# A two-layer transformer block on one core: the half-empty last chunk of the first MLP packed two ways, and the order of weight splits and maxima beside it

## The chip, the cores and the metric

One NeuronCore of one Trainium2 chip runs the whole program. The metric is device time in microseconds (us) of that core. The kernel before was run three times: 1961.26, 1966.72 and 1971.39 us, median 1966.72 us.

## The reference, cut to what matters

Four residual sublayers follow one another: attention with 16 heads of 128, a gated MLP, causal attention with 16 heads of 16, a mixture of experts. Each normalises its input and its output. The change lies in the second, and in the preparation of the third that runs beside it.

```
x = x + _layernorm(_L0_attn_ref(_layernorm(x), ...))
x = x + _layernorm(_L0_ffn_ref(_layernorm(x), ...))
x = x + _layernorm(_L1_attn_ref(_layernorm(x), ...))
x = x + _layernorm(_L1_ffn_ref(_layernorm(x), ...))

def _L0_ffn_ref(x, gate_w, up_w, down_w, gate_s, up_s, down_s):   # 2048 tokens, 256 features, INTER = 704
    g = jnp.einsum('th,ih->ti', xf, gate_w) * gate_s
    u = jnp.einsum('th,ih->ti', xf, up_w) * up_s
    hdn = jax.nn.silu(g) * u
    out = jnp.einsum('ti,hi->th', hdn, down_w) * down_s
```

## The kernel before, in words

Everything is fp32. A product of two fp32 tensors is done as three matmuls of rounded parts (high by high, high by low, low by high; `PASSES`, function `project`, line 81), each operand being held as a pair `_hi`, `_lo`.

The first MLP (`Mlp0.block`) works in 24 steps s = 0 to 23. Step s takes the 512 tokens of chunk c = s // 6 and the hidden units of part e = s % 6, 128 at a time. The 704 hidden units are five parts of 128 and one of 64: for e = 5 (steps 5, 11, 17 and 23) the other 64 units are zeros. Within a step:

- TensorE, `gate_up(s)`: 6 matmuls of 512 columns for the gate into one PSUM bank, 6 for the up projection into the next (line 81).
- ScalarE, `silu(s)` (L1369): 128x512, as soon as the gate is there.
- VectorE, `product(s)` (L1451): silu times up, 128x512.
- ScalarE, `split_hidden(s)` (L1376): the high part `mlp_hid_hi`.
- GpSimd (L1426): the low part `mlp_hid_lo`.
- TensorE, `down(s)`: 8 matmuls of 256 columns with the high part (L1333), then 4 with the low part (L1337), added up in two banks of PSUM over the six steps of a chunk. Step 0 of a chunk first writes zeros into the banks (L1330).

TensorE issues `gate_up(s + 1)` ahead of `down(s)`, so that the other engines have the time of `gate_up(s + 1)` to make the hidden values of step s.

```
gate_up(0)
for s in range(STEPS):
    gate_up(s + 1)
    early.tensor(pe, s, 0)
    down(s)
    turn(...)                  # X_TURN, NEXT_TURN
    early.tensor(pe, s, 1)
```

Each engine runs its program in the order of the code. Other work is set into the steps by tables: the norm before (`before`: X_ADD, X_STATS, X_ACT, X_TURN), the norm after (`after`: NEXT_ACC, NEXT_ADD, NEXT_STATS, NEXT_X_ACT, NEXT_TURN), the splits of the MLP's own weights (`SPLIT`, L1362 on ScalarE and L1417 on GpSimd), and class `Early`, which prepares the next attention. For this text the following of it count:

- On GpSimd, `Early.gpsimd` splits weights into high and low parts: in step 6 those of query and key (`split_weights`), in step 8 both halves of the value weights (`halve`, L2015 and L2017), in steps 9 and 11 those of the output weights (L2148, L2151). In step 8 they follow `scale_x` of the norm (L216 to L221).
- In steps 16 to 23 TensorE computes the first scores of the next attention just for their row maxima (`early_jobs`, L2058 with the mask L2065, 64 rows each, in pairs over the two halves of the array), and VectorE reduces them (`take_max`, L2091 and L2094; here called peaks). Two banks are used in turn, so that each pair of scores waits for the peaks before it. "when" 0 stands ahead of `down(s)`, "when" 1 behind it.
- VectorE does the peaks of step s - 1 in its pass s (`early.vector(dve, s - 1)`), behind `product(s)` and behind `take_lo` (L379), which takes the low part of a tile that TensorE has transposed (`turn`, L365) and of which ScalarE has first taken the high part (L370).

## Time and profile before

| | |
|---|---|
| runs | 1961.26, 1966.72, 1971.39 us |
| the profiled execution's own time | 1961.52 us |
| its span | 1959.7 us, mean granted clock of TensorE 0.985 |
| TensorE matmuls busy | 1864.2 us (95%) |
| TensorE weight loads busy | 1471.1 us (75%) |
| VectorE busy | 1429.8 us (73%) |
| ScalarE busy | 1176.6 us (60%) |
| GpSimd busy | 1173.6 us (60%) |

The program is a sequence of stages: the first attention to about 1135 us of the span, the first MLP from there to about 1271 us, then the second attention and the experts. The page's rows of engine activity are means over slices of 49 us, so the MLP is less than three of them; it has to be read in finer stretches. Matmul durations in the trace include the time that a matmul takes to run through the array: consecutive ones overlap, and what one costs in a row of them is the distance from start to start.

### The profile page before, as it was taken

Reading aid. Unit: us, or ns where it says so; the run is one execution under the profiler, and the core shown is the slowest. Engines: PE = TensorE matmul, PEld = TensorE weight load, DVE = VectorE, ACT = ScalarE, POOL = GpSimd, SP = SyncE. Lnnn points to the kernel's source line nnn. Section 1 sums busy time; section 2 is a strip of 40 time slices with the busy share of each in tenths; the row PEclk is TensorE's granted clock in tenths of the full one; section 3 lists DMA queues with packets and bytes.
Section 4 is the critical chain, followed back from the end, with each engine's and each line's share of the span. In section 5 each row is a group of like instructions: output and inputs, shape, how many; then the busy total and the mean of one; then the engine's idle time right before and its main releaser. Section 6 shows DMA issues by size and latency. Waiting matters only on the chain. (4 is left out here: it accounts for less than half of the span.)

```text
span 1959.7 us, 31266 instructions
## 1 busy us (share of the span) xinstructions
PE 1864.2 (95%) x10576; PEld 1471.1 (75%) x10576; DVE 1429.8 (73%) x2312; ACT 1176.6 (60%) x1897; POOL 1173.6 (60%) x945
## 2 busy tenths in 40 slices
PE   6999999999999999999999699889999989999997
PEld 5778888888888888888888577654555546888886
DVE  7777888888888888888888644377777766655556
ACT  5666676666666766666666655257666765533333
POOL 3776776777777767867766665214434446554445
PEclk9999999999999999999999899989999999999999
DMA  7877777778677777777777420000000010110001
GB/s 210 278 256 265 269 269 280 256 270 283 246 271 275 264 260 258 268 283 259 269 271 260 159 87 1 2 12 4 4 4 4 2 49 25 41 41 25 17 1 44
DMA packets 195603, 310.68 MB, mean 159 GB/s; under 512 B 12080, under 2 KB 154160, under 8 KB 195504
## 3 DMA queue, kind: packets, MB, share of 16 engines
q1 hardware_dynamic: 195504, 309.39, 45.9%
q8 instruction: 59, 0.97, 0.2%
q14 instruction: 40, 0.33, 0.1%
HBM read 173.03 MB, written 136.31 MB: 158 GB/s over the span
## 5 line engine op out<-in xcount | busy, mean ns | idle before, releaser
L620 POOL TENSOR_TENSOR attn_probT_lo<-attn_probT_lo,attn_probT_hi 128x1024 fp32r<-128x1024 f32 x254 | 610.6, 2404 | 198.4 <-ACT attn_probT_hi L987 198.1
L1104 DVE STREAM_TRANSPOSE attn_turned_prob<-attn_prob 128x1024 f32<-128x1024 f32 x256 | 318.2, 1243 | 123.9 <-ACT attn_prob L977 65.2
L977 ACT ACTIVATE attn_prob<-psum,attn_neg_max 128x1024 f32<-128x1024 f32 x256 | 285.7, 1116 | 145.2 <-DVE attn_neg_max L1098 142.0
L1098 DVE TENSOR_REDUCE attn_neg_max<-psum 128x1 f32<-128x1024 f32 x256 | 305.8, 1195 | 18.6 <-PE psum L81 18.0
L987 ACT ACTIVATE attn_probT_hi<-attn_probT_lo 128x1024 fp32r<-128x1024 f32 x256 | 269.3, 1052 | 2.2 <-DMA attn_probT_lo<-attn_spill 2.1
L81 PE MATMUL psum<-attn_probT_hi,attn_v_hi 128*128 128x512 f32 x512 | 205.5, 401 | 21.9 <-POOL attn_probT_lo L620 20.2
L81 PE MATMUL psum<-attn_probT_lo,attn_v_hi 128*128 128x512 f32 x512 | 205.3, 401 | 0.0
L81 PE MATMUL psum<-attn_key_hi,attn_q_hi 128*128 128x512 f32 x512 | 200.6, 392 | 3.8 <-ACT attn_prob L977 2.2
L81 PE MATMUL psum<-attn_probT_hi,attn_v_lo 128*128 128x512 f32 x512 | 203.6, 398 | 0.0
L81 PE MATMUL psum<-attn_key_lo,attn_q_hi 128*128 128x512 f32 x512 | 201.9, 394 | 0.0
L81 PE MATMUL psum<-attn_key_hi,attn_q_lo 128*128 128x512 f32 x512 | 201.2, 393 | 0.0
L2094 DVE TENSOR_REDUCE attn_peaks<-psum 128x1 f32<-128x512 f32 (+1 forms) x256 | 156.0, 652 | 45.3 <-PE psum L2065 30.0
L1718 POOL TENSOR_TENSOR attn_qk_lo<-attn_moe_hidden,attn_qk_hi 128x512 fp32r<-128x512 f32 (+1 forms) x73 | 93.6, 1282 | 142.8 <-ACT attn_qk_hi L1660 142.8
L2546 ACT ACTIVATE attn_probT<-psum 128x512 f32<-128x512 f32 (+1 forms) x256 | 129.1, 574 | 40.6 <-PE psum L2428 34.9
L830 POOL TENSOR_TENSOR attn_v_lo<-attn_v_whole,attn_v_hi 128x512 fp32r<-128x512 f32 x64 | 83.3, 1301 | 104.0 <-ACT attn_v_hi L999 103.7
L1747 DVE TENSOR_TENSOR attn_moe_hidden<-psum,attn_v 128x512 f32<-128x512 f32 (+1 forms) x73 | 49.8, 683 | 115.5 <-ACT attn_v L1653 109.0
L81 PEld LDWEIGHTS psum<-attn_probT_hi,attn_v_hi 128*128 128x128 f32 x512 | 97.0, 189 | 44.3 <-issue 14.4
L81 PEld LDWEIGHTS psum<-attn_key_hi,attn_q_hi 128*128 128x128 f32 x512 | 96.6, 189 | 29.2 <-ACT attn_prob L977 3.5
L2364 POOL TENSOR_SCALAR_AFFINE_SELECT attn_probT<-attn_probT 128x256 f32<-128x256 f32 x128 | 52.0, 420 | 110.7 <-ACT attn_probT L2546 56.7
L81 PE MATMUL psum<-xT_hi,attn_w_hi 128*128 128x512 f32 x288 | 116.6, 405 | 1.4 <-ACT attn_probT L2546 0.5
L81 PE MATMUL psum<-xT_hi,attn_w_lo 128*128 128x512 f32 x288 | 114.7, 398 | 0.0
L81 PEld LDWEIGHTS psum<-attn_probT_hi,attn_v_lo 128*128 128x128 f32 x512 | 97.1, 190 | 23.5
(251 smaller groups left out, 4761.1 us busy)
## 6 DMA issues: line engine op xcount, KB each, us to landing
attn_spill<-attn_turned_prob SPq DMA_DIRECT2D x256, 512.0 KB, 4.5
attn_probT_lo<-attn_spill SPq DMA_DIRECT2D x256, 512.0 KB, 5.0
x_sb<-in_w_qkvo SPq DMA_DIRECT2D x30, 512.0 KB, 5.0
attn_v_all<-in_moe_w SPq DMA_DIRECT2D x24, 384.0 KB, 3.0
acc_sb<-in_x SPq DMA_DIRECT2D x4, 512.0 KB, 6.1
acc_sb<-in_bo SPq DMA_DIRECT2D x16, 128.0 KB, 6.9
x_sb<-in_x SPq DMA_DIRECT2D x4, 512.0 KB, 5.5
mlp_staged<-in_ffn_w SPq DMA_DIRECT2D x4, 384.0 KB, 4.9
```

The costliest lines, as they stand in the source:

```text
L81: ins = nc.tensor.matmul(out, stationary[s], moving[m], start=start and n == 0, stop=stop and n == len(PASSES) - 1)
L620: engine.tensor_tensor(lo, f32(lo), f32(hi), ALU.subtract).then_inc(done, 1)
L830: nc.gpsimd.tensor_tensor(v[1][:, to, cols], v_whole[:, to, cols], f32(v[0][:, to, cols]), ALU.subtract).then_inc(v_done, 1)
L977: nc.scalar.activation(prob[:, tile % 2, :].rearrange("p (b n) -> p b n", b=NSQ), by_key, ACT.Exp, bias=neg_max[:, tile % 2:tile % 2 + 1], ...
L987: nc.scalar.activation(hi, f32(lo), ACT.Copy).then_inc(hi_done, 1)
L1098: nc.vector.tensor_reduce(neg_max[:, tile % 2:tile % 2 + 1], scores(tile), AX.XY, ALU.max, negate=True).then_inc(max_ready, 1)
L1104: nc.vector.transpose(turned_prob[:, tile % 2, :], prob[:, tile % 2, :]).then_inc(turned, 1)
L1718: self.nc.gpsimd.tensor_tensor(self.hid[1][p % 2][:, at], self.hidden[p % 2][:, at], f32(self.hid[0][p % 2][:, at]), ALU.subtract).then_in ...
L1747: self.nc.vector.tensor_tensor(self.hidden[p % 2][:, at], self.k.psum[:, self.slots[p % 2][1], at], self.gate_act[p % 2][:, at], ALU.mult) ...
L2094: nc.vector.tensor_reduce(to[:, h:h + 1], bank[:, 0:width], AX.X, ALU.max, negate=True).then_inc(max_free, 1)
L2364: nc.gpsimd.affine_select(out=at, in_=at, pattern=[[0, 2], [1, P]], compare_op=ALU.is_ge, fill=0.0, base=0, channel_multiplier=-1).then_in ...
L2546: nc.scalar.activation(probT[:, slot(g, h), q0:], score_bank(g, h), ACT.Exp, scale=float(D1) ** -0.5).then_inc(exp_done, 1)
```

## The change

Three things are changed.

1. In the steps with e = 5 (`narrow`), gate and up weights of the 64 units stand side by side in one stationary of 128 columns. The first 256 tokens of the chunk go through [gate, up] into one bank, the other 256 through [up, gate] into the other: 12 matmuls of 256 columns. Silu and product are each done in two instructions of 64x256, the product reading the up values in the other half of the partitions than the one it writes. The hidden values of the first 256 tokens then lie in partitions 0 to 63, of the other 256 in 64 to 127, in 256 columns; the split into high and low is 128x256. The down projection has 12 matmuls of 64 rows, alternately in the upper and the lower half of the rows, each pair into the two banks.
2. On GpSimd the value weights are split in steps 9 and 11, the output weights in steps 12 and 14.
3. On VectorE the peaks of the "when" 0 scores come ahead of `take_lo`, and in a narrow step ahead of the product.

```diff
@@ Mlp0.block
+        HALF_NB = NB // 2
+        sides = (slice(0, P // 2), slice(P // 2, P))
+        narrow = lambda s: part_of(s) == N - 1
@@ gate_up
+                    if narrow(s):
+                        for half, (cols_of, full) in enumerate(((gates, gate_full), (ups, up_full))):
+                            at = slice(c * NB + half * HALF_NB, c * NB + (half + 1) * HALF_NB)
+                            project(nc, banks[:, half, 0:HALF_NB], cols_of, lambda kt: [h[:, kt, at] for h in k.xT]).then_inc(full, 1)
+                        return
@@ down
+                def narrow_down(c, buffer, weights, lo_of):
+                    for j in range(GT // 2):
+                        for of, weight in ((0, 0), (0, 1)) if lo_of is None else ((lo_of, 0),):
+                            for side in range(2):
+                                mm = nc.tensor.matmul(down_tile(c, side * GT // 2 + j), hid[of][sides[side], buffer, j * P:(j + 1) * P],
+                                                      weights[weight][sides[side], :], start=False, stop=of == 1 and j == 1)
+                    return mm
+                    if narrow(s):
+                        narrow_down(c, s % 2, weights, lo_of=None)
+                        pe.wait_ge(lo_done, s + 1)
+                        narrow_down(c, s % 2, weights, lo_of=1).then_inc(down_full, 1)
+                        return
@@ silu
+                    if narrow(s):
+                        for side in range(2):
+                            if side:
+                                act.wait_ge(up_full, s + 1)
+                            nc.scalar.activation(gate_act[sides[side], s % 2, 0:HALF_NB],
+                                                 slot(("step", s))[sides[side], side, 0:HALF_NB], ACT.Silu,
+                                                 scale=scales[sides[side], 0, e:e + 1]).then_inc(silu_done, 1)
+                        return
@@ product
+                    if narrow(s):
+                        e = part_of(s)
+                        for side in range(2):
+                            dve.wait_ge(silu_done, silus_before(s) + side + 1)
+                            mul = nc.vector.scalar_tensor_tensor(out=hidden[sides[side], s % 2, 0:HALF_NB],
+                                                                 in0=slot(("step", s))[sides[1 - side], side, 0:HALF_NB],
+                                                                 scalar=scales[sides[side], 1, e:e + 1],
+                                                                 in1=gate_act[sides[side], s % 2, 0:HALF_NB], op0=ALU.mult, op1=ALU.mult)
+                        mul.then_inc(prod_done, 1)
+                        return
@@ VectorE, pass s
+                    if narrow(s):
+                        early.vector(dve, s - 1, 0)
                     product(s)
...
                     if s - 1 in X_TURN:
                         before.take_lo(dve, X_TURN[s - 1], slot(("x", X_TURN[s - 1])))
+                    if not narrow(s):
+                        early.vector(dve, s - 1, 0)
                     if s - 1 in NEXT_TURN:
                         after.take_lo(dve, NEXT_TURN[s - 1], slot(("next", NEXT_TURN[s - 1])))
-                    early.vector(dve, s - 1)
+                    early.vector(dve, s - 1, 1)
@@ Early.gpsimd
-                if step == 8:
+                if step == 9:
                     pool.wait_ge(wv_landed, 32)
-                    halve(pool, wv_in[:], [flat(h[:]) for h in wv], wv_ready, 2)
-                if step == 9:
+                    nc.gpsimd.tensor_tensor(flat(wv[0][:]), wv_in[:], one[:].broadcast_to([P, KC * C]), ALU.mult).then_inc(split, 1)
+                if step == 11:
+                    pool.wait_ge(split, 2)
+                    nc.gpsimd.tensor_tensor(flat(wv[1][:]), wv_in[:], f32(flat(wv[0][:])), ALU.subtract).then_inc(wv_ready, 1)
+                if step == 12:
                     nc.gpsimd.tensor_tensor(flat(wp[0][:]), wp_in[:], one[:].broadcast_to([P, passes // 2 * C]), ALU.mult).then_inc(split, 1)
-                if step == 11:
+                if step == 14:
```

The weights are arranged on the host, outside the measured time: the last chunk of `ffn0_w` holds [gate, up], [up, gate] and the 64 rows of down twice, and its scales stand in both halves.

**GpSimd, steps 8 to 11.** `mlp_hid_lo` is the low part of a step's hidden values; the four `room_sb` rows are `scale_and_offset` of a norm. Before:

```order
L216 TENSOR_SCALAR room_sb<-room_sb 128x4
L217 TENSOR_SCALAR room_sb<-room_sb 128x4
L219 TENSOR_TENSOR room_sb<-room_sb 128x4
L221 TENSOR_TENSOR room_sb<-room_sb 128x4
L2015 TENSOR_TENSOR attn_wv_hi<-attn_in_wv,attn_one 128x512
L2017 TENSOR_TENSOR attn_wv_lo<-attn_in_wv,attn_wv_hi 128x512
L1426 TENSOR_TENSOR mlp_hid_lo<-mlp_hidden,mlp_hid_hi 128x512
L2148 TENSOR_TENSOR attn_wp_hi<-attn_in_wp,attn_one 128x512
L1426 TENSOR_TENSOR mlp_hid_lo<-mlp_hidden,mlp_hid_hi 128x512
```

and now (L1458 is L1426 of before, L2193 makes the high part of the value weights, L2196 the low part):

```order
L221 TENSOR_TENSOR room_sb<-room_sb 128x4
L1458 TENSOR_TENSOR mlp_hid_lo<-mlp_hidden,mlp_hid_hi 128x512
L2193 TENSOR_TENSOR attn_wv_hi<-attn_in_wv,attn_one 128x512
L1458 TENSOR_TENSOR mlp_hid_lo<-mlp_hidden,mlp_hid_hi 128x512
L216 TENSOR_SCALAR room_sb<-room_sb 128x4
L217 TENSOR_SCALAR room_sb<-room_sb 128x4
L219 TENSOR_TENSOR room_sb<-room_sb 128x4
L221 TENSOR_TENSOR room_sb<-room_sb 128x4
L1458 TENSOR_TENSOR mlp_hid_lo<-mlp_hidden,mlp_hid_hi 128x256
L2196 TENSOR_TENSOR attn_wv_lo<-attn_in_wv,attn_wv_hi 128x512
```

The low part of step 9 no longer has two splits ahead of it, and that of step 11 has 256 columns.

**VectorE, steps 17 to 19.** Before, where L1451 is the product, L379 is `take_lo` and L2091 and L2094 are peaks:

```order
L2091 TENSOR_REDUCE attn_peaks<-psum 128x2 x2
L2094 TENSOR_REDUCE attn_peaks<-psum 128x1 x2
L1451 SCALAR_TENSOR_TENSOR mlp_hidden<-psum,mlp_in_scales,mlp_gate_act 128x512
L379 TENSOR_TENSOR xT_lo<-psum,xT_hi 128x2x512
L2094 TENSOR_REDUCE attn_peaks<-psum 128x1 x4
```

and now (L2138 and L2141 are the peaks, L1485 the two halves of a narrow product, L1493 a whole one):

```order
L2138 TENSOR_REDUCE attn_peaks<-psum 128x2 x2
L1485 SCALAR_TENSOR_TENSOR mlp_hidden<-psum,mlp_in_scales,mlp_gate_act 64x256 x2
L2141 TENSOR_REDUCE attn_peaks<-psum 128x1 x2
L1493 SCALAR_TENSOR_TENSOR mlp_hidden<-psum,mlp_in_scales,mlp_gate_act 128x512
L2141 TENSOR_REDUCE attn_peaks<-psum 128x1 x2
L379 TENSOR_TENSOR xT_lo<-psum,xT_hi 128x2x512
L2141 TENSOR_REDUCE attn_peaks<-psum 128x1 x2
```

Two of the four peaks that stood behind `take_lo` now stand ahead of it, and the first pair stands ahead of the product of step 17.

**TensorE, step 5.** The down projection of a narrow step now (L1333 is `narrow_down`; "x2" is one matmul in each half of the rows). Before, these were 8 and 4 single matmuls over all 128 rows:

```order
L1333 MATMUL psum<-mlp_w_hi,mlp_hid_hi 128x256 x2
L1333 MATMUL psum<-mlp_w_lo,mlp_hid_hi 128x256 x2
L1333 MATMUL psum<-mlp_w_hi,mlp_hid_hi 128x256 x2
L1333 MATMUL psum<-mlp_w_lo,mlp_hid_hi 128x256 x2
L1333 MATMUL psum<-mlp_w_hi,mlp_hid_lo 128x256 x4
```

There are as many matmuls as before, in six pairs.

## Rows read from the trace of the kernel before

**Rows 1.** Busy time by stretch: us, each engine's busy time, TensorE's granted clock, DMA
```profile
1235.00:1240.00 5.00, 4.57 (x15) 3.39 (x16) 1.40 (x3) 0.69 (x1) 0.00 (x0) 0.50 0.00 0
...
1290.00:1300.00 10.00, 9.62 (x63) 6.31 (x65) 4.90 (x10) 6.65 (x12) 2.68 (x5) 0.66 0.00 0
```

**Rows 2.** Timeline, TensorE, steps 9 and 10: start us, us, engine, line, what
```profile
1180.37 0.40 PE L81 MATMUL psum<-xT_hi,mlp_w_hi 128*128 128x512 f32 x1
...
1182.94 0.40 PE L81 MATMUL psum<-xT_hi,mlp_w_lo 128*128 128x512 f32 x1
1183.17 0.28 PE L1333 MATMUL psum<-mlp_w_hi,mlp_hid_hi 128*128 128x256 f32 x1
...
1184.00 0.28 PE L1333 MATMUL psum<-mlp_w_lo,mlp_hid_hi 128*128 128x256 f32 x1
```

**Rows 3.** Timeline, GpSimd, step 4
```profile
1158.66 1.84 POOL L1417 TENSOR_TENSOR mlp_w_lo<-x_sb,mlp_w_hi 128x768 fp32r<-128x768 f32 x1
```

**Rows 4.** Timeline, TensorE, into matmuls of 64 rows and back (PEld: weight loads)
```profile
1212.87 0.64 PE L1337 MATMUL psum<-mlp_w_hi,mlp_hid_lo 128*128 128x256 f32 x4
1213.44 0.19 PEld L2039 LDWEIGHTS psum<-attn_qk_hi,attn_to_stack 64*128 64x128 f32 x2
1213.44 0.50 PE L2039 MATMUL psum<-attn_qk_hi,attn_to_stack 64*128 64x512 f32 x2
1213.78 0.40 PE L2039 MATMUL psum<-attn_qk_lo,attn_to_stack 64*128 64x512 f32 x2
1214.11 0.50 PE L81 MATMUL psum<-xT_hi,mlp_w_hi 128*128 128x512 f32 x1
1214.45 0.40 PE L81 MATMUL psum<-xT_lo,mlp_w_hi 128*128 128x512 f32 x1
```

**Rows 5.** Timeline, GpSimd and TensorE, step 9
```profile
1182.85 2.11 POOL L2015 TENSOR_TENSOR attn_wv_hi<-attn_in_wv,attn_one 128x512 fp32r<-128x512 f32 x1
1185.04 1.27 POOL L2017 TENSOR_TENSOR attn_wv_lo<-attn_in_wv,attn_wv_hi 128x512 fp32r<-128x512 f32 x1
1186.27 1.27 POOL L1426 TENSOR_TENSOR mlp_hid_lo<-mlp_hidden,mlp_hid_hi 128x512 fp32r<-128x512 f32 x1
...
1187.59 0.74 PE L1337 MATMUL psum<-mlp_w_hi,mlp_hid_lo 128*128 128x256 f32 x4 [3.32 <-POOL mlp_hid_lo L1426]
```

**Rows 6.** Timeline, ScalarE, steps 9 and 10
```profile
1184.91 0.67 ACT L1369 ACTIVATE mlp_gate_act<-psum,mlp_in_scales 128x512 f32<-128x512 f32 x1
1186.40 0.63 ACT L1376 ACTIVATE mlp_hid_hi<-mlp_hidden 128x512 fp32r<-128x512 f32 x1 [0.82 <-DVE mlp_hidden L1451]
```

**Rows 7.** Groups of instructions in the MLP, GpSimd: count, busy us, mean ns, idle before
```profile
L1426 POOL TENSOR_TENSOR mlp_hid_lo<-mlp_hidden,mlp_hid_hi 128x512 fp32r<-128x512 f32 x24 | 32.4, 1349 | 54.3 <-ACT mlp_hid_hi L1376 54.1
```

**Rows 8.** Timeline, VectorE, steps 18 and 19
```profile
1228.77 0.75 DVE L1451 SCALAR_TENSOR_TENSOR mlp_hidden<-psum,mlp_in_scales,mlp_gate_act 128x512 f32<-128x512 f32 x1 [1.77 <-ACT mlp_gate_act L1369]
...
1232.96 1.23 DVE L379 TENSOR_TENSOR xT_lo<-psum,xT_hi 128x1024 fp32r<-128x1024 f32 x1 [3.44 <-ACT xT_hi L370]
1234.10 1.28 DVE L2094 TENSOR_REDUCE attn_peaks<-psum 128x1 f32<-128x512 f32 x2
```

**Rows 9.** Timeline, TensorE, steps 17 and 18: scores for maxima, then gate of step 19
```profile
1225.04 0.50 PE L2058 MATMUL psum<-attn_key,attn_q 64*128 64x512 f32 x2 [0.40 <-DVE attn_peaks L2091]
...
1235.43 0.69 PE L2058 MATMUL psum<-attn_key,attn_q 64*128 64x384 f32 x2 [3.70 <-DVE attn_peaks L2094]
...
1236.29 0.79 PE L81 MATMUL psum<-xT_hi,mlp_w_hi 128*128 128x512 f32 x1
...
1240.88 0.40 PE L81 MATMUL psum<-xT_hi,mlp_w_lo 128*128 128x512 f32 x1
```

**Rows 10.** Groups of instructions in the MLP, VectorE: count, busy us, mean ns
```profile
L2094 DVE TENSOR_REDUCE attn_peaks<-psum 128x1 f32<-128x512 f32 x8 | 5.1, 685 | 2.4 <-PE psum L2058 1.6 <-PE psum L2065 0.7
...
L2091 DVE TENSOR_REDUCE attn_peaks<-psum 128x2 f32<-128x256 f32 x2 | 0.7, 416 | 0.0
```

**Rows 11.** Timeline, TensorE, last step
```profile
1267.80 0.50 PE L2058 MATMUL psum<-attn_key,attn_q 64*128 64x512 f32 x2 [1.38 <-DVE attn_peaks L2094]
```

More of the change, by code:

```diff
@@ L1241, in block @@
         chunk_of = lambda s: s // N
+        HALF_NB = NB // 2
+        sides = (slice(0, P // 2), slice(P // 2, P))
+        narrow = lambda s: part_of(s) == N - 1
+        tokens_of = lambda s: HALF_NB if narrow(s) else NB
+        silus_before = lambda s: s + s // N
         X_ADD, X_STATS, X_ACT, X_TURN = {3: 2, 7: 3}, {4: 2, 8: 3}, {5: 2, 9: 3}, {7: 2, 11: 3}
@@ L1313, in gate_up @@
                     banks = slot(("step", s))
-                    project(nc, banks[:, 0, :], lambda kt: weights(slice(kt * IM, (kt + 1) * IM)),
-                            x).then_inc(gate_full, 1)
-                    project(nc, banks[:, 1, :], lambda kt: weights(slice(cols_up + kt * IM, cols_up + (kt + 1) * IM)),
-                            x).then_inc(up_full, 1)
+                    gates = lambda kt: weights(slice(kt * IM, (kt + 1) * IM))
+                    ups = lambda kt: weights(slice(cols_up + kt * IM, cols_up + (kt + 1) * IM))
+                    if narrow(s):
[3 more added lines that the diff above has]
+                        return
+                    project(nc, banks[:, 0, :], gates, x).then_inc(gate_full, 1)
+                    project(nc, banks[:, 1, :], ups, x).then_inc(up_full, 1)
+                def narrow_down(c, buffer, weights, lo_of):
[5 more added lines that the diff above has]
+                    return mm
                 def down(s):
@@ L1375, in split_hidden @@
                         act.wait_ge(down_full, s - 1)
-                    nc.scalar.activation(hid[0][:, s % 2, :], hidden[:, s % 2, :], ACT.Copy).then_inc(hi_done, 1)
+                    nc.scalar.activation(hid[0][:, s % 2, 0:tokens_of(s)], hidden[:, s % 2, 0:tokens_of(s)], ACT.Copy).then_inc(hi_done, 1)
                 def copy_out(c):
@@ L1425, in _ @@
                     pool.wait_ge(hi_done, s + 1)
-                    nc.gpsimd.tensor_tensor(hid[1][:, s % 2, :], hidden[:, s % 2, :], f32(hid[0][:, s % 2, :]),
+                    of = slice(0, tokens_of(s))
+                    nc.gpsimd.tensor_tensor(hid[1][:, s % 2, of], hidden[:, s % 2, of], f32(hid[0][:, s % 2, of]),
                                             ALU.subtract).then_inc(lo_done, 1)
@@ L1479, in _ @@
                         after.stats_x(dve, NEXT_STATS[s])
-                early.vector(dve, STEPS - 1)
+                for when in range(2):
+                    early.vector(dve, STEPS - 1, when)
 class Moe:
@@ L2200, in scalar, with vector @@
                             take_stack(act, 0, n, part, bank)
-            def vector(self, dve, step):
-                if step == 8:
+            def vector(self, dve, step, when):
+                if step == 8 and when == 0:
                     dve.wait_ge(consts, 64)
@@ L2210, in vector @@
                     dve.wait_ge(prepared, 2)
-                for job in self.done_in(step):
+                for job in early_jobs.get(step, ((), ()))[when]:
                     kind, n, part = job
@@ L2764 @@
                               pad_hidden(given["L0_ffn_down_w"].T))
+    last, own = arrays["ffn0_w"][-1], IM // 2
+    in_gate, in_up = (last[:, n * KC * IM:(n + 1) * KC * IM].reshape(P, KC, IM)[:, :, 0:own] for n in range(2))
+    arrays["ffn0_w"][-1] = np.concatenate([
+        np.concatenate([in_gate, in_up], axis=2).reshape(P, -1), np.concatenate([in_up, in_gate], axis=2).reshape(P, -1),
+        np.concatenate([last[0:own, 2 * KC * IM:], last[0:own, 2 * KC * IM:]])], axis=1)
     arrays["ffn0_scales"] = np.stack([pad_hidden(given[f"L0_ffn_{n}_s"]).reshape(N_FFN0, IM).T for n in ("gate", "up")])
+    arrays["ffn0_scales"][:, own:, -1] = arrays["ffn0_scales"][:, 0:own, -1]
     arrays["down_s"] = given["L0_ffn_down_s"]
```

4 lines of the change are left out of this document (2 added, 2 removed).

## The prediction

> **What bounds the kernel now.** The page comes first, and says little here: TensorE's matmuls are busy 95% of the span, and the change touches the MLP alone, 136 us of it. I read that stage by stretches of 5 us. TensorE has 5.00 us busy in most of them, and the exceptions are what a reader should look for: a wait in step 9, one in step 17 with a granted clock of 0.50 behind it [rows 1], and short waits at the end. Then the timeline of TensorE. Twelve matmuls of 512 columns run from 1180.37 to 1182.94, (2.57 / 11 =) 0.234 us each from start to start; eight of 256 columns from 1183.17 to 1184.00, (0.83 / 7 =) 0.119 each [rows 2]. These distances, not the durations of 0.40 and 0.28 in the same rows, are what a matmul costs. A step is 12 x 0.234 + 12 x 0.119 = 4.2 us of TensorE, and as long as nothing is late TensorE is the bound of this stage. So the sum is TensorE time removed, plus waits removed, minus waits that appear.
>
> All positions below are those of the trace of before.
>
> **A, gate and up.** Each narrow step has 12 matmuls of 256 instead of 512 columns: 12 x (0.234 - 0.119) = 1.4 us, four times 5.5. One small loss: gate and up of step 6 need weights whose low part ends on GpSimd at 1158.66 + 1.84 = 1160.50 [rows 3]; TensorE would now be there at 1160.35. 0.2 is taken off: **5.3 us**.
>
> **B, down.** Six pairs instead of twelve matmuls. That two matmuls of 64 rows run side by side is in the trace: the pair at 1213.44 (row x2) is followed by the next at 1213.78, and that one by the next matmul at 1214.11, so two times 512 columns take 0.33, which two in turn (0.47) would not fit into. Both weight loads of a pair are over in 0.19, the length of one [rows 4]. So 6 x 0.119 = 0.71 is saved. Against it stands going from 128 rows to 64 and back. The four matmuls at 1212.87 should be followed after 4 x 0.119 at 1213.34, the pair starts at 1213.44; the next follows after 0.34 rather than 0.234: 0.10 + 0.10. On the way back 0.33 and 0.34 stand for 0.234 again. One change of size costs 0.20 [rows 4]. Steps 5 and 11 gain such a change in both directions: 0.71 - 0.41 = 0.3 each. In steps 17 and 23 the scores ahead of the down are of 64 rows already, so the change moves behind the down in 17 (0.71) and falls away in 23 (0.9). Sum **2.2 us**. Bounds: 3.0 gained, if the change of size were hidden; 0.6 lost, if the pairs ran in turn (2.2 - 4 x 0.71). I take the value by the pairs of 512 columns, the nearest row.
>
> The rule in the Trainium skill, TensorEngine Tiling (Array Packing), Key Properties, is that changing the tiling mode drains TensorE; it gives no price. It speaks against part B, and the trace agrees with 0.20 a time. The same skill's TensorE: Matmul & The Clock Gate, LDWEIGHTS, says that a load costs its columns, whatever its rows: 107 ns for 128 columns by its formula, an estimate, so that pairs whose two loads came one after the other would cost 0.21 and B would be nothing.
>
> **C, the value weights.** The low part of step 9 starts at 1186.27, behind splits of 2.11 and 1.27 us, and TensorE waits 3.32 [rows 5]. Without them GpSimd gets to it when the norm's small work ends, at 1182.85, and is done at 1184.12; TensorE wants it at 1184.00 + 0.12 [rows 2]. The 3.3 go. Next late is step 10. Its silu starts at 1184.91, because the norm's work on ScalarE stands ahead of it; its high part is done at 1186.40 + 0.63 = 1187.03 [rows 6]. That chain moves with TensorE, which is 1.5 earlier by then (1.2 + 0.3 of step 5): 1185.5. TensorE, after down(9) ending at 1183.1 and a gate and up of step 11 of only 1.4, is there at 1184.5: it waits 1.0, and about 0.4 more for the low part, which needs 1.27 [rows 5] where the high matmuls give 0.95 of cover. **3.3 - 1.4 = 1.9 us.** Before, the wait for step 9 hid this. The splits that move to steps 9, 11, 12 and 14 take 1.3 to 2.1 each; GpSimd idles 54.3 us ahead of the 24 low parts, over 2 us a step [rows 7], and in step 11 its own low part is half as long; nobody reads them before the next stage. Cost nothing; if one fell ahead of a low part that TensorE awaits, at most 1.3 each.
>
> **D, the maxima.** VectorE ends the product of step 18 at 1229.5 and then stands 3.44 in front of `take_lo`, until the transposed tile's high part is there; the peaks behind it were ready all along, end at 1235.4, and TensorE waits 3.70 for them [rows 8, 9]. Now they run from 1229.5 to 1230.8, when TensorE is still in the transposes: 3.6 go. Behind the wait the granted clock was 0.50 of full, the lower level of 1.2 GHz [rows 1]: gate and up of step 19 took from 1236.29 to 1240.88, 0.417 a matmul for 0.234 [rows 9], and the scores ahead of them 0.86 to the next start for 0.65. That gives back 2.0 + 0.2. Peaks before the product of step 17 also take away the 0.40 in front of the second scores [rows 9]. What is late next: the peaks behind `take_lo`, which down(18) needs. After the turn come the high part (1.0), `take_lo` (1.23) and peaks of 384 columns (1.0, between the two rows of peaks), while TensorE has 0.65 of scores and 2.8 of gate and up: no wait, by some 0.2. **6.2 us.**
>
> **E, the small engines.** Two half products for one: by the nearest row of a half-width reading of PSUM, 416 ns against 685 [rows 10], about 0.5 each for 0.75 [rows 8]: 0.2 more on VectorE; two half silus, 0.3 more on ScalarE, less 0.2 for the shorter high part; GpSimd is relieved of 0.6 a step. Bounds: 0.37 and 0.75 per half. The cover is gate and up of the wide step that follows, 2.8 us, which stays. Step 23 has only the scores' wait as cover [rows 11], where VectorE is free before the scores are. **0.**
>
> **The sum** is 5.3 + 2.2 + 1.9 + 6.2 = 15.6 us. What lies behind the MLP starts on a barrier and moves forward as a whole. The profiled execution took 1961.5 us, so 1945.9 by its own time; the median of the three runs lies 5.2 above. I take the median less the sum, **1951 us**.
>
> What no row can fix: where the half-level stretches behind the MLP fall. 1290 to 1300 is at 0.66 [rows 1]: (1.00 - 0.66) x 2 = 0.68 of the time at half speed, at most 3.4 us of cost. Everything arrives there 15.6 us earlier, so up to 4 more or less.
>
> **The rivals.**
>
> 1. *The pairs run in turn.* Pairs of 512 columns speak against it [rows 4]; with 256 each load has half the time to hide in. B becomes -0.6, the time 1954. By the skill's rule on loads it would be 1953. Chance 0.10.
> 2. *The clock falls anyway.* The new wait of 1.4 us in step 10, or the shorter work of the narrow steps, puts a stretch at half speed elsewhere. For it: in this stage 3.7 us of wait was enough; against: the wait of 3.32 in step 9 was followed by no fall. One or two such stretches cost 2.2 each, one behind the stage up to 3.4: 1953 to 1957, say 1956. Chance 0.15.
> 3. *The cover is gone.* In each narrow step the others have 1.4 us less to bring the hidden values of the step before, and TensorE waits where it computed: all of A is given back except what C has counted. 15.6 - 3.9 = 11.7, 1955. For it: step 10, where I find it. Against: VectorE and ScalarE idle before their part of most steps. Chance 0.12.
> 4. *Slower.* Half-filled matmuls, two a pair with 64 rows each, keep TensorE so little occupied that the granted clock goes to its lower level from the first narrow step on. Work of X us at full clock then costs X more, so the gain is used up when 15.6 us of work, some 31 us of the stage, run at 0.50. If all the work from step 5 to the end did, about 95 us, it would be 1951 + 95 = 2046 us. Against it: the downs of 256 columns keep their 0.119 at full clock [rows 2], and the narrow downs are 4 x 1 us. The point for slower by over 0.5% is 51 us at 0.50. Chance 0.03.
>
> That the change does not do what it says has little room: the order of instructions shows six pairs and the moved peaks; what is left is rival 1.
>
> **How the numbers follow.** My forecast has 0.60. Before's three runs lie 0.5% apart, which is also what a measurement of this kernel can tell from no change: faster by over 0.5% is below 1956.9. Of the forecast 0.55 falls there (the sum would have to be off by 6 us), of rival 1 0.09, of 2 0.09, of 3 0.08: 0.81. Slower 0.03, the rest 0.16. The range takes the sum with the unfixed 4 us and the lowest of the runs downwards (1961.3 - 19.6 = 1942), and upwards rivals 1 to 3 with the bounds: 1960.
>
> **What would show it.** Matmuls of 256 columns on line 81 in four groups of 12 at 0.119; down of a narrow step in 1.1 us; no wait of TensorE for the low part of step 9, but one of 1 to 1.4 in step 10; no wait of several us between the transposes of step 17 and the next scores, and a clock of 1.00 there; the MLP 15 to 16 us shorter from its first matmul to the barrier. A MLP shortened by less than 11, or a clock of 0.50 inside it, makes the sum wrong; a MLP shortened as said with the time elsewhere makes the whole wrong and the parts right.

## The result, and the profile after

The changed kernel takes 1946.63 us, the median of four runs (1943.77 to 1950.39), beside 1969.06 (1961.26 to 1974.59) for four of the kernel before; the ratio is 0.9888, interval 0.9866 to 0.991. Run again on another chip it takes 1951.99 beside 1967.88, ratio 0.9906, 0.9883 to 0.9928. Forecast were 1951 and a range of 1942 to 1960.

| | before | after |
|---|---|---|
| the profiled execution's own time | 1961.52 us | 1944.76 us |
| span, mean granted clock | 1959.7, 0.985 | 1943.0, 0.987 |
| first matmul of the MLP to gate of step 5 | 22.28 | 23.44 |
| gate of step 5 to the barrier | 113.78 | 98.30 |
| ahead of the MLP, behind it | 1135.2, 688.5 | 1134.9, 686.4 |

The last three lines come from the timelines; the MLP's first matmul starts at 1135.19 us before and at 1134.85 after. Of the kernel after, the first narrow matmul on TensorE, and SyncE's first transfer behind the barrier that ends the MLP:

```profile
1158.29 0.36 PE L81 MATMUL psum<-xT_hi,mlp_w_hi 128*128 128x256 f32 x1 [0.32 <-issue]
...
1256.59 0.33 SPq L2374 DMA_DIRECT2D attn_sum_rows<-in_sum_rows  x1
```

The kernel before has the same two points in its timeline:

```profile
1157.47 0.47 PE L81 MATMUL psum<-xT_hi,mlp_w_hi 128*128 128x512 f32 x1 [0.23 <-issue]
...
1271.25 0.33 SPq L2324 DMA_DIRECT2D attn_sum_rows<-in_sum_rows  x1
```

98.30 for 113.78 is **15.5 us less, where the sum said 15.6**. This distance, called the changed stretch below, holds all that the change touches. It is also the steady measure: in the second execution of the change it is 98.33. What lies around it is the same code in both kernels and varies by itself: the MLP starts at 1134.5 to 1139.1 in the profiled executions, its head takes 22.2 to 22.3 us in most of them and 23.4 to 23.6 in others, whatever the kernel, and what lies behind takes 686.4 to 694.3.

The whole MLP, for which the prediction named 15 to 16 us less, went from 136.1 to 121.7, so 14.3 shorter; in the second execution it is 120.6, 15.5 shorter. The first one's head stands in part at the lower clock, ahead of everything that the change touches:

```profile
1135.00:1140.00 5.00, 5.00 (x16) 3.94 (x17) 3.10 (x10) 1.36 (x2) 3.94 (x8) 0.66 0.83 274
```

The kernel before and the second execution have 1.00 in their heads. The five engine values in such a row are the busy times of TensorE, its weight loads, VectorE, ScalarE and GpSimd; the number behind them is the granted clock.

The waits of TensorE in the changed stretch, in the kernel before (us in total, times, longest):

```profile
PE psum L2058 <- DVE attn_peaks L2094: 5.1, 2, 3.7
PE psum L1337 <- POOL mlp_hid_lo L1426: 3.3, 1, 3.3
...
PE psum L2058 <- DVE attn_peaks L2091: 0.4, 1, 0.4
```

and in the kernel after (L2141 is L2094 of before, L1458 is L1426):

```profile
PE psum L2105 <- DVE attn_peaks L2141: 1.4, 1, 1.4
PE psum L1360 <- POOL mlp_hid_lo L1458: 1.1, 2, 0.9
```

3.3 and 3.7 us of wait are gone. What has come is 1.1 us for GpSimd's low parts. In windows of 5 us the stretch behind the scores of steps 17 and 18, which answers to the 0.50 of [rows 1], stands at full clock:

```profile
1225.00:1230.00 5.00, 4.85 (x27) 3.35 (x25) 2.90 (x4) 3.06 (x4) 0.72 (x1) 1.00 0.00 0
1230.00:1235.00 5.00, 5.00 (x38) 3.84 (x38) 1.27 (x3) 0.89 (x2) 1.29 (x1) 1.00 0.00 0
```

The timeline of TensorE in step 5 has the narrow down, where a wide step has eight single matmuls ([rows 2] show them) and four. The row ahead is the last of gate and up of step 6, the rows behind are the first of step 7:

```profile
1164.00 0.40 PE L81 MATMUL psum<-xT_hi,mlp_w_lo 128*128 128x512 f32 x1
1164.33 0.39 PE L1333 MATMUL psum<-mlp_w_hi,mlp_hid_hi 64*128 64x256 f32 x2
1164.55 0.28 PE L1333 MATMUL psum<-mlp_w_lo,mlp_hid_hi 64*128 64x256 f32 x2
1164.67 0.28 PE L1333 MATMUL psum<-mlp_w_hi,mlp_hid_hi 64*128 64x256 f32 x2
1164.79 0.28 PE L1333 MATMUL psum<-mlp_w_lo,mlp_hid_hi 64*128 64x256 f32 x2
1164.90 0.40 PE L1333 MATMUL psum<-mlp_w_hi,mlp_hid_lo 64*128 64x256 f32 x4
1165.23 0.50 PE L81 MATMUL psum<-xT_hi,mlp_w_hi 128*128 128x512 f32 x1
1165.57 0.39 PE L81 MATMUL psum<-xT_lo,mlp_w_hi 128*128 128x512 f32 x1
```

Read the distances of starts: 0.12 from pair to pair. Four distances are about 0.1 longer than their matmuls ask, two on the way in (0.33 for 0.234, 0.22 for 0.119) and two on the way out (0.33 for the last two pairs' 0.24, 0.34 for 0.234). From 1164.00 to 1165.57 there are 1.57 us; two matmuls of 512 columns are 0.47 of it, so the down costs 1.10. Before it was 12 x 0.119 = 1.43.

The timelines of GpSimd and VectorE in step 9, and TensorE's two waits:

```profile
1180.45 1.53 POOL L219 TENSOR_TENSOR room_sb<-room_sb 128x4 f32<-128x4 f32 x1
1182.06 0.20 POOL L221 TENSOR_TENSOR room_sb<-room_sb 128x4 f32<-128x4 f32 x1
1182.21 2.34 POOL L1458 TENSOR_TENSOR mlp_hid_lo<-mlp_hidden,mlp_hid_hi 128x512 fp32r<-128x512 f32 x1
...
1182.20 1.23 DVE L275 TENSOR_TENSOR x_sb<-x_sb,acc_sb 128x1024 f32<-128x1024 f32 x1
```

```profile
1184.61 0.74 PE L1360 MATMUL psum<-mlp_w_hi,mlp_hid_lo 128*128 128x256 f32 x4 [0.94 <-POOL mlp_hid_lo L1458]
...
1187.87 0.74 PE L1360 MATMUL psum<-mlp_w_hi,mlp_hid_lo 128*128 128x256 f32 x4 [0.15 <-POOL mlp_hid_lo L1458]
```

GpSimd starts the low part as forecast, right behind the norm's small work. But it takes 2.34 us for the 1.27 of [rows 5], while VectorE's addition of 1.23 us (L275) runs beside it.

The trace of before had a sign of this. There the same addition ran beside the first split, whose 2.11 us stand in [rows 5], and an operation of the same kind and shape without the addition beside it took half of that:

```profile
1182.84 1.22 DVE L275 TENSOR_TENSOR x_sb<-x_sb,acc_sb 128x1024 f32<-128x1024 f32 x1
...
1187.50 1.04 POOL L2148 TENSOR_TENSOR attn_wp_hi<-attn_in_wp,attn_one 128x512 fp32r<-128x512 f32 x1
```

### The profile page after: what moved, and what is told of

Read it like the earlier page. It is cut to its first block and busy times, and to the rows that moved or that the text cites. A ratio compares the mean times of both kernels' runs of the same rounds, so it can differ in the third digit from the quotient of the medians.

```text
span 1943.0 us, 31274 instructions
## 1 busy us (share of the span) xinstructions
PE 1855.7 (96%) x10576; PEld 1463.3 (75%) x10576; DVE 1431.3 (74%) x2316; ACT 1175.5 (60%) x1901; POOL 1169.9 (60%) x945
## 5 line engine op out<-in xcount | busy, mean ns | idle before, releaser
L2141 DVE TENSOR_REDUCE attn_peaks<-psum 128x1 f32<-128x512 f32 (+1 forms) x256 | 155.9, 651 | 44.4 <-PE psum L2112 29.8
L81 PEld LDWEIGHTS psum<-attn_probT_hi,attn_v_lo 128*128 128x128 f32 x512 | 97.2, 190 | 23.6
L81 PE MATMUL psum<-xT_hi,attn_q 128*128 128x512 f32 x288 | 114.6, 398 | 0.0
```

Source lines behind the costliest of these rows:

```text
L81: ins = nc.tensor.matmul(out, stationary[s], moving[m], start=start and n == 0, stop=stop and n == len(PASSES) - 1)
L2141: nc.vector.tensor_reduce(to[:, h:h + 1], bank[:, 0:width], AX.X, ALU.max, negate=True).then_inc(max_free, 1)
```

## The experiments

Each is measured in the changed stretch too, against the change's 98.3.

**The change once more.** Edit: none.

> The change as it is, once more beside the kernel before. In the profiles the first MLP (first matmul to the start of the next stage's first transfer) went from 136.1 to 121.7 us and the span by 16.7, yet the medians differ by 22.4. Theory 1: the change is worth its sum of 15.6 and about 1 us more, the rest is scatter of the kernel before: ratio 0.9915, 16 to 18 us. Theory 2: about 5 us more come from outside of the MLP: ratio 0.9888, and the stretch behind the MLP is shorter by over 4 us.

1951.99 us, ratio 0.9906 (0.9883 to 0.9928), nearer to the first theory's 0.9915 than to the second's 0.9888; changed stretch 98.33. So the stretch repeats within 0.1 us, while the two profiled executions differ by 8 us in all: 4.3 ahead of the MLP, 4.7 behind it, and 1.2 the other way in its head. For what lies behind, windows of both show a difference: the change's first profile, then this one, each 1260 to 1300.

```profile
1260.00:1300.00 40.00, 33.84 (x268) 20.25 (x268) 30.12 (x61) 24.25 (x45) 7.34 (x16) 1.00 0.06 13
```

```profile
1260.00:1300.00 40.00, 34.67 (x240) 22.77 (x240) 27.88 (x55) 18.37 (x33) 7.38 (x16) 0.87 0.08 15
```

A granted clock of 1.00 or 0.87 over 40 us, for one and the same program, is up to 0.13 x 40 = 5.2 us, enough for the 4.7. What made the 4.3 ahead of the MLP stays open.

**Part 1 undone: the last 64 units as before.**

```diff
-        narrow = lambda s: part_of(s) == N - 1
+        narrow = lambda s: False
+        last_part = lambda s: part_of(s) == N - 1
...
-        silus_before = lambda s: s + s // N
+        silus_before = lambda s: s
```

The peaks keep their places of part 3 (by `last_part` instead of `narrow`), and the weights' old arrangement comes with it.

> Part 1 of the change undone (last 64 units as a full chunk with zeros), parts 2 and 3 kept. The sum says A + B = 5.3 + 2.2 = 7.5 us longer than the change; the MLP lasts 121.7 + 7.5 = 129 us, TensorE waits in steps 9 and 10 as long as in the change (1.1 in all) or less. Rival, cover gone: the narrow steps are bounded by the other engines, so that undoing them costs under 5 us.

1956.45 us, ratio 0.9938 (0.9917 to 0.996); changed stretch 105.90, 7.6 more than the change. That looks like A + B, which was 7.5, to the tenth, and isn't quite. In the last 4 us before the barrier this execution has a low clock, which the change has not:

```profile
1260.05:1262.05 2.00, 2.00 (x12) 1.78 (x11) 1.29 (x2) 0.00 (x0) 0.00 (x0) 0.70 0.00 0
1262.05:1264.05 2.00, 0.68 (x4) 0.39 (x2) 0.00 (x0) 1.02 (x1) 0.00 (x0) 0.50 0.00 0
```

From the last scores to the barrier are 4.21 us, in the kernel before, at full clock, 3.45 (1267.80 to 1271.25): 0.8 of the 7.6 are clock, and 6.8 the change's own. Followed step by step from the gate of step 5, the two timelines part by 1.4 at each narrow gate and up of steps 17 and 23, by 0.7 at the down of 17, 0.9 at that of 23, 1.45 over step 5, all as forecast, but by 0.96 over step 11 where 1.7 was forecast. 0.3 of what is missing is the low part of step 10, which C has counted. Most of the rest is a wait of 0.35 that only the change has, on the weight loads ahead of the matmuls behind the turn of step 11:

```profile
1196.56 0.19 PEld L81 LDWEIGHTS psum<-xT_hi,mlp_w_hi 128*128 128x128 f32 x1 [0.35 <-DVE mlp_hidden L1493]
```

(second execution of the change). Gate and up of step 13 need the banks that VectorE's product of step 12 still reads.

This run also has 0.9 us of wait for the low part of step 9, as the change has: that wait does not come from the narrow steps.

**Part 2 undone: the value and output weights split in steps 8, 9 and 11.**

```diff
-                if step == 9:
+                if step == 8:
                     pool.wait_ge(wv_landed, 32)
-                    nc.gpsimd.tensor_tensor(flat(wv[0][:]), wv_in[:], one[:].broadcast_to([P, KC * C]), ALU.mult).then_inc(split, 1)
-                if step == 11:
...
+                    halve(pool, wv_in[:], [flat(h[:]) for h in wv], wv_ready, 2)
+                if step == 9:
```

> Part 2 undone (value weights split whole in step 8, output weights in 9 and 11). TensorE waits 3 to 4 us for the low part of step 9 again instead of 0.94, and no longer in step 10: 2 to 3 us longer than the change, MLP 124 us. Rival: the wait comes back but narrow steps behind it take it up, under 1 us.

1956.15 us, ratio 0.9934 (0.9915 to 0.9953); changed stretch 101.59, 3.3 more. TensorE's timeline and the windows behind the wait:

```profile
1189.12 1.17 PE L1360 MATMUL psum<-mlp_w_hi,mlp_hid_lo 128*128 128x256 f32 x4 [3.45 <-POOL mlp_hid_lo L1458]
```

```profile
1185.00:1190.00 5.00, 1.55 (x10) 1.34 (x9) 2.17 (x6) 3.28 (x6) 4.92 (x5) 0.92 0.00 0
1190.00:1195.00 5.00, 5.00 (x31) 4.83 (x29) 1.68 (x8) 2.08 (x5) 3.62 (x7) 0.74 0.00 0
```

A wait of 3.45 for 1.09 is 2.4 of the 3.3. The clock fell behind this wait: the two rows lose up to 1.7 us to it, and by the starts of both timelines it cost 1.5. In all, by the starts, 3.3 is 2.5 for the wait in step 9 and 1.5 for the clock, less 0.4 in step 10 and the product's 0.35, which the longer wait covers. In the kernel before the clock had not fallen behind 3.32.

**Part 3 undone: the peaks behind `take_lo` and behind the product.**

```diff
-                    if narrow(s):
-                        early.vector(dve, s - 1, 0)
                     product(s)
...
-                    if not narrow(s):
-                        early.vector(dve, s - 1, 0)
...
+                    early.vector(dve, s - 1, 0)
                     early.vector(dve, s - 1, 1)
```

> Part 3 undone (all maxima behind take_lo and behind the product). TensorE waits about 3.7 us for the peaks in step 17 again. Theory 1, the wait brings the lower clock with it: 0.50 behind it and 5.5 to 6.2 us longer than the change, MLP 127.5 us. Rival: the clock fell in the kernel before by where it happened to stand; then the clock stays 1.00 and it is 3.6 to 4 us longer.

1960.55 us, ratio 0.996 (0.9942 to 0.9978); changed stretch 106.60, 8.3 more. On TensorE's timeline, and in the windows:

```profile
1223.37 0.50 PE L2102 MATMUL psum<-attn_key,attn_q 64*128 64x512 f32 x2 [2.01 <-DVE attn_peaks L2135]
1233.04 0.69 PE L2102 MATMUL psum<-attn_key,attn_q 64*128 64x384 f32 x2 [3.70 <-DVE attn_peaks L2138]
```

```profile
1230.00:1235.00 5.00, 1.96 (x9) 1.37 (x10) 3.42 (x5) 1.38 (x2) 0.00 (x0) 0.71 0.00 2
1235.00:1240.00 5.00, 5.00 (x14) 3.37 (x13) 0.66 (x2) 0.69 (x1) 0.00 (x0) 0.61 0.00 0
```

5.7 us of wait, and the clock behind it for most of the other 2.6 (2.4 by the starts). Forecast were 5.5 to 6.2 in all. The 3.70 is that of [rows 9] to the hundredth. The wait in step 17 is 2.01, where before it was 0.40: in a narrow step TensorE is there 1.4 sooner, while the silu stays behind the norm's work on ScalarE (L261, 2.07), and from the first silu's start to the peaks it is 1.58 with the halves and was 1.37 with the whole. 0.40 + 1.4 + 0.2 is 2.0. So the place ahead of the product is worth five times what the prediction gave it, once the step is narrow.

**Part 1 alone.** Edit: those of parts 2 and 3 undone together.

> Part 1 alone, parts 2 and 3 undone. Theory, the parts add up: 7.5 us less than the kernel before in the MLP (136.1 to 128.6), with waits of 3.3 to 3.5 in step 9 and 3.7 in step 17 as before. Rival: since the narrow product now stands ahead of the first peaks, another 2.0 us of wait in front of the second scores, as in the run with late maxima: 6 us less.

1961.79 us, ratio 0.9958 (0.9943 to 0.9973); changed stretch 111.08, only 2.7 less than before, where A + B by itself would be 7.5 and the rival gave 6. The windows say where the rest went, the steps behind step 9 first and then those from 17 on:

```profile
1185.00:1190.00 5.00, 3.44 (x17) 3.45 (x18) 2.42 (x10) 1.10 (x2) 4.84 (x7) 0.66 0.00 0
1220.00:1225.00 5.00, 2.99 (x25) 2.19 (x24) 2.35 (x5) 2.27 (x6) 0.72 (x1) 0.88 0.00 0
1225.00:1230.00 5.00, 5.00 (x28) 3.77 (x30) 1.94 (x3) 0.80 (x2) 0.00 (x0) 0.78 0.02 3
1230.00:1235.00 5.00, 1.31 (x14) 0.94 (x10) 2.42 (x3) 2.46 (x3) 1.26 (x1) 0.91 0.00 2
1235.00:1240.00 5.00, 4.99 (x16) 3.72 (x17) 1.02 (x2) 0.69 (x1) 0.00 (x0) 0.50 0.00 0
1240.00:1245.00 5.00, 5.00 (x29) 3.52 (x28) 1.73 (x3) 0.63 (x1) 1.28 (x1) 0.91 0.00 0
```

The waits are 3.28, 2.01 and 3.70, so 1.6 more in step 17 than before. A stretch of 5 us at a mean clock f loses up to 5 x (1 - f): here the six rows lose up to 6.8 us; before, stretches at 0.87, 0.50 and 0.95 (1230 to 1245) lost up to 3.4. The difference of these two bounds is 3.4; with the 1.6 that makes 5.0 for the missing 4.8, and by the starts, stretch for stretch against before, it is 1.6 and 3.2. A new wait and the clock took most of the gain.

**The pairs written in turn: first all matmuls of one half of the rows, then all of the other.**

```diff
-                    for j in range(GT // 2):
-                        for of, weight in ((0, 0), (0, 1)) if lo_of is None else ((lo_of, 0),):
-                            for side in range(2):
+                    for side in range(2):
+                        for j in range(GT // 2):
+                            for of, weight in ((0, 0), (0, 1)) if lo_of is None else ((lo_of, 0),):
```

> The narrow down projection with all matmuls of the upper 64 rows ahead of all of the lower (6 and 6 matmuls in a row instead of six pairs: 4 and 4 high, 2 and 2 low). Theory, pairs run side by side: now they mostly don't, 12 x 0.119 plus the changes of size instead of 6 x 0.119, so 0.6 to 0.7 us more in each of four steps, 2.5 to 2.8 us in the MLP (from 120.6 to 123.2). Rival, what part B gained is the number of rows and not the pairing: no change.

1951.84 us, ratio 0.9924 (0.9903 to 0.9944); changed stretch 98.53, 0.2 more. The order of TensorE's instructions is really in turn; against the change's (cut after the first four of one half):

```
-L1333 MATMUL psum<-mlp_w_hi,mlp_hid_hi 128x256 x2
-L1333 MATMUL psum<-mlp_w_lo,mlp_hid_hi 128x256 x2
...
+L1333 MATMUL psum<-mlp_w_hi,mlp_hid_hi 128x256
+L1333 MATMUL psum<-mlp_w_lo,mlp_hid_hi 128x256
+L1333 MATMUL psum<-mlp_w_hi,mlp_hid_hi 128x256
+L1333 MATMUL psum<-mlp_w_lo,mlp_hid_hi 128x256
```

and yet its timeline has them side by side, at the distances of the change:

```profile
1163.44 0.40 PE L1333 MATMUL psum<-mlp_w_hi,mlp_hid_hi 64*128 64x256 f32 x2
1163.67 0.29 PE L1333 MATMUL psum<-mlp_w_lo,mlp_hid_hi 64*128 64x256 f32 x2
...
1164.36 0.50 PE L81 MATMUL psum<-xT_hi,mlp_w_hi 128*128 128x512 f32 x1
```

So the edit did not make what it was meant to make, and it says nothing on what pairing is worth. It shows that matmuls in the other half of the rows start ahead of their turn: the fifth of the program starts with the first. For the price another kernel was needed.

**All narrow downs in the first half of the rows.** This one computes something else: for the second 256 tokens it uses the first 256 tokens' hidden values again.

```diff
-    hid[of][sides[side], buffer, j * P:(j + 1) * P],
-    weights[weight][sides[side], :]
+    hid[of][sides[0], buffer, j * P:(j + 1) * P],
+    weights[weight][sides[0], :]
```

> The four narrow downs use the first 64 rows of the hidden values and of the down weights for both halves of the tokens, so the second 256 tokens' part of it is left out and the first 256 tokens' part is used twice: twelve matmuls in one and the same half of the rows, no two in different ones. If two halves of the rows run beside each other, whatever their order in the program, this takes six more matmul pitches of 0.119 us per step: 0.71 in each of four steps, 2.85 in all, so the MLP takes 123.4 to 123.6 us where the change has 120.6 to 121.7 (the third step's is beside nothing; in step 23 it is on the path too). Rival, the row halves never ran beside each other (the two starts recorded as one are only how the records are made): no difference in the MLP, 120.6 to 121.7, and 0.119 between the starts of pairs was a pitch of single matmuls.

One run, 1950.66 us; changed stretch 100.80, 2.5 more, against 2.85 expected. (The whole MLP has 124.4, above the 123.4 to 123.6 expected, as its head took 23.6.) Its timeline:

```profile
1165.18 0.50 PE L1333 MATMUL psum<-mlp_w_hi,mlp_hid_hi 64*128 64x256 f32 x2
1165.52 0.40 PE L1333 MATMUL psum<-mlp_w_lo,mlp_hid_hi 64*128 64x256 f32 x2
...
1166.80 0.50 PE L81 MATMUL psum<-xT_hi,mlp_w_hi 128*128 128x512 f32 x1
```

The "x2" here are two in turn: behind the way in, the next stands 0.24 later, in rows left out here too, where the pairs had 0.12. From the first to line 81 there are 1.62 us for 0.90. The 0.72 is the six pitches of 0.119 that the pairs save. Four times that is 2.9; in step 11 the longer down hides the 0.35 that TensorE would wait for the product, which is no longer among its waits, and 2.5 remain. Rival 1 is out: the halves do run beside each other.

**VectorE's casts one step earlier**, since they and the addition stand beside GpSimd's work in step 9.

```diff
-                if step == 8 and when == 0:
+                if step == 7 and when == 0:
```

> VectorE's five constants of the next attention (1.9 us of casts) moved from pass 9 into pass 8, where it idles 2.6 us ahead of take_lo. Theory, GpSimd's low part of step 9 took 2.34 us instead of 1.29 because VectorE's addition of 1.23 us ran at the same time: now the addition runs earlier, beside the norm's small work, the low part takes 1.3 and TensorE's wait of 0.94 to 1.0 in step 9 goes, while step 10 waits 1.0 to 1.4 as the prediction said: MLP the same within 0.4. Rival, the low part is slow for another reason: 2.3 us again.

One run, 1953.4 us; changed stretch 100.65, 2.3 more: worse. The addition moved forward with the casts, and came to lie beside the norm's L219:

```profile
1180.78 2.07 POOL L219 TENSOR_TENSOR room_sb<-room_sb 128x4 f32<-128x4 f32 x1
...
1183.08 1.26 POOL L1458 TENSOR_TENSOR mlp_hid_lo<-mlp_hidden,mlp_hid_hi 128x512 fp32r<-128x512 f32 x1
```

The low part is down to 1.26, as the theory had it. But L219 is up from 1.53 to 2.07, and L216, which begins the chain, starts 1.8 later in the stretch, since the norm's statistics on VectorE now stand behind the casts. The expectation of no difference was wrong by that. TensorE waits 1.64 and 0.30 in step 9 and 0.81 in step 10.

**The addition alone one step later.**

```diff
-        NEXT_ACC, NEXT_ACC_ACT, NEXT_ADD = {7: 0, 13: 1}, {8: 0, 14: 1}, {9: 0, 15: 1}
+        NEXT_ACC, NEXT_ACC_ACT, NEXT_ADD = {7: 0, 13: 1}, {8: 0, 14: 1}, {10: 0, 15: 1}
```

> VectorE's addition of 1.2 us for the next chunk stands one step later, in step 10, so that it no longer lies beside GpSimd's low part of step 9. If GpSimd's low part is slower because of VectorE beside it, it falls from 2.34 to about 1.3 us, TensorE's wait in step 9 from 0.94 to nothing, and the low part of step 10 (now the one beside the addition, and behind a gate and up that comes 0.9 sooner) makes it wait 0.9 to 1.4. Sum within 0.5 us of the change: MLP 120.3 to 121.5. Rival, the 2.34 us come from something else of step 9 (its weights' split ahead of it, or the casts): the low part stays at 2.2 to 2.4 and the wait at 0.9.

One run, 1951.61 us; changed stretch 99.43, 1.1 more, where at most 0.5 was expected. GpSimd's timeline has the low parts of steps 9 and 10, TensorE's the waits:

```profile
1181.85 1.29 POOL L1458 TENSOR_TENSOR mlp_hid_lo<-mlp_hidden,mlp_hid_hi 128x512 fp32r<-128x512 f32 x1
...
1186.28 1.54 POOL L1458 TENSOR_TENSOR mlp_hid_lo<-mlp_hidden,mlp_hid_hi 128x512 fp32r<-128x512 f32 x1 [2.13 <-ACT mlp_hid_hi L1407]
```

```profile
1186.26 0.39 PE L1356 MATMUL psum<-mlp_w_hi,mlp_hid_hi 128*128 128x256 f32 x1 [0.90 <-ACT mlp_hid_hi L1407]
1187.87 0.74 PE L1360 MATMUL psum<-mlp_w_hi,mlp_hid_lo 128*128 128x256 f32 x4 [0.40 <-POOL mlp_hid_lo L1458]
```

With the addition gone from beside it the low part of step 9 takes 1.29, the wait there is gone, and the next low part, beside the addition's end, takes 1.54. In its place stand 0.90 and 0.40 in step 10, **which is the wait the prediction had put there** (1.0 and 0.4). The wait for the product of step 12 grows too, from 0.35 to 0.83: the addition's norm reaches ScalarE 1.1 later, ahead of the silu that this product needs. That part is the price of the new place, not of the forecast picture.

**Two attempts at a better kernel.** The first: casts as above, the norm's ScalarE work in step 10 instead of 9, and the first scores of the last group ahead of the down of step 22, with their peaks behind the product of step 23.

```diff
-        X_ADD, X_STATS, X_ACT, X_TURN = {3: 2, 7: 3}, {4: 2, 8: 3}, {5: 2, 9: 3}, {7: 2, 11: 3}
+        X_ADD, X_STATS, X_ACT, X_TURN = {3: 2, 7: 3}, {4: 2, 8: 3}, {5: 2, 10: 3}, {7: 2, 11: 3}
...
-                    if narrow(s):
+                    if narrow(s) and s < 20:
                         early.vector(dve, s - 1, 0)
...
-                    if not narrow(s):
+                    if not narrow(s) or s > 20:
                         early.vector(dve, s - 1, 0)
...
-        22: ([], [("max", 4, 0)]),
+        22: ([("max", 4, 0)], []),
...
-                if step == 8 and when == 0:
+                if step == 7 and when == 0:
```

> As e6, and besides the norm's work on ScalarE moved from step 9 behind the silu of step 10, and the first scores of the last group moved ahead of the down of step 22, with their peaks behind the product of step 23. Theory: no wait in steps 9 and 10 (1.0 us), and 0.7 us less at the end: MLP 119 us, 1.5 to 1.7 less than the change (120.6). Too little for the times to show. Rival: the norm's work comes too late and step 11 or 12 waits instead, 0.7 only.

1952.1 us, ratio 0.9922 (0.9906 to 0.9938); changed stretch 99.48, 1.2 more, where 1.5 to 1.7 less was expected. Of the last maximum's wait of 1.38 only 0.4 is left, but 1.65 are waited in step 9, much as in the run with the casts early, here with a clock of 0.73 and 0.93 in the ten microseconds around it, up to 1.7 us.

The second keeps the casts where the change has them and moves the addition as above, with the other two edits.

> The change, with the addition in step 10 as in e10, the norm's ScalarE part one step later (behind silu(10), so that GpSimd's low part of step 10 is not late), and the last maximum ahead of the product in step 22 as in e7. If the waits are what the rows show, 0.94 in step 9, 0.15 in step 10 and 1.38 in the last step all go: MLP 2 to 2.5 us shorter than the change's 120.6 to 121.7, so 118.5 to 119.5. Rival, each wait removed is taken up by the next late operation on GpSimd or ScalarE, as in e7 (121.7): MLP 120.5 or more, no difference in the time. The whole time's own scatter of some us outside the MLP can hide 2 us in the median.

1945.44 us (1940.81 to 1948.94) beside 1970.58, ratio 0.9872 (0.9848 to 0.9895); changed stretch 96.99, **1.3 less than the change**, where 2 to 2.5 was expected. TensorE's remaining waits for the low parts and for peaks:

```profile
PE psum L1360 <- POOL mlp_hid_lo L1458: 0.5, 1, 0.5
...
PE psum L2105 <- DVE attn_peaks L2141: 0.4, 1, 0.4
```

0.9 us where the change has 2.5. Of GpSimd's work it is now the value weights' split that lies beside the addition, and takes 2.02 for 1.03, where nobody waits for it. The ratio's interval overlaps those of the change (up to 0.991 and 0.9928 from 0.9866 and 0.9883), so that it beats the change is shown for the stretch, not for the whole time.

## Why the prediction was right

- **A, gate and up, 5.3, and B, down, 2.2: right but for step 11.** 6.8 by undoing them, 7.1 with the 0.3 that C had counted. The pitch of 0.119 for 256 columns and the change of size came out as [rows 4] had them for pairs of 512 columns: 1.10 us for the down of step 5, where 6 x 0.119 + 0.41 is 1.12. The Trainium skill's rule that a change of tiling mode drains TensorE (TensorEngine Tiling (Array Packing), Key Properties) agrees with this trace: 0.20 for the way in and 0.20 for the way out. That the two loads of a pair come one after the other, the prediction's second price for rival 1, is out too: it asked for 0.21 a pair, and the pairs stand 0.12 apart.
- **C, the value weights, 1.9: right in size, wrong in its path.** 3.3 left and 1.1 came as waits (1.25 by the starts: in step 10 the low matmuls are due at 1187.56 and start at 1187.87), so 2.1; undoing it brought 2.4 of wait. But the step that said "GpSimd is done at 1184.12" took 1.27 for the low part, as if GpSimd's durations did not depend on VectorE. It took 2.34, TensorE waited 0.94 in step 9, and that delay gave step 10 the time it lacked: 0.15 instead of 1.4. Moving the addition brought the forecast picture back, with 1.3 in step 10. Two errors of about one microsecond cancelled, since both stand in the same chain of waits: that is luck. The 2.11 of [rows 5] beside the 1.04 of L2148 could have told.
- **D, the maxima, 6.2: right from before's side.** The waits of 3.70 and 0.40 and the clock of 0.50 are gone, and no wait of a like size has come: by the starts 4.2 of wait and 2.1 behind it, where the sum had 4.0 and 2.2. The zeros of step 18 wait about 0.2 for peaks, as the sum allowed. From the change's side the same edit is worth 8.3, since a narrow step 17 makes 2.0 out of the 0.40. The prediction priced the peaks ahead of the product in a wide step.
- **E, the small engines, 0: 0.35.** Half a product is 483 ns and half a silu 465 in their groups, within the bounds of 0.37 and 0.75. The cover named, gate and up of the wide step behind, was enough for hidden values. But TensorE also waits for PSUM banks that the product reads, and there the shorter down of step 11 uncovered 0.35.
- **The sum, 15.6 against 15.5.** Laid side by side from the gate of step 5, the starts of before and after give C 2.1 (2.4 gained in step 9, 0.3 lost in step 10), D 6.3, and all the rest, A + B less the 0.35 of E, 7.1 where A + B was 7.5. The errors are -0.4, 0.2 and 0.1. No term is far off, but that they add up to a tenth is luck, and so is the way C came to its size.
- **The rivals.** 1 is refuted by the kernel with one half of the rows. 2 did not happen in the changed stretch, where both executions of the change have 1.00 throughout (the 0.66 of the first stands in the head), but it is real: behind waits of 3.45, 3.28 and 1.65 the clock fell in experiments. 3 was right only in step 10 and behind step 11, for 0.3 and 0.35 us; the 0.94 of step 9 is there with wide steps too. 4 has nothing for it: the clock is 1.00 through all narrow steps.
- **The level.** The first series lies 4.4 us below the forecast of 1951, the second 1.0 above. The unfixed 4 us were meant for this: in the 40 us behind the MLP the clock was 1.00 in one execution and 0.87 in another of one program. Why it differs stays open.

## What to carry to other kernels

Parts of a change that take work from the bounding engine and parts that take waits from it are not additive: part 1 alone brought 2.7 of its 7.5 us, because the waits and the low clock behind them took the rest. So shorten the work and clear the next waits together, and judge in a stretch whose ends you can name in both traces; here it repeats within 0.1 us, while the whole time moves by several.

Before you give an operation of GpSimd the duration of its group, look at what VectorE will run beside it in the new order.
